# Scan layers of a four-layer kernel: B turned four times a pass, its diagonals made by VectorE straight from the scratch bank, and the second half's fills in another order

## The reference

```python
proj = seq @ W_proj.T + b_proj                     # x_in, delta, B, C
delta = softplus(delta + dt_bias)
h = exp(d_t * A) * h + (d_t * x_t) * b_t           # over the 1024 tokens, per channel and state
y_t = einsum('bdn,bn->bd', h, c_t)                 # C picks out of the 16 states
out = (y + x_in * D) @ W_out.T + b_out
```

## Time and profile before

| | |
|---|---|
| median of 3 runs | 4393.69 us (4382.99 to 4408.94) |
| the profiled execution | 4387.91 us, its span 4386.1 us |
| scans of the scan layers (line 1111) | first at 1808.9 us, last at 4361.1 us |
| PE busy | 3855.6 us, 88% |
| DVE busy | 3288.3 us, 75% |
| POOL busy | 2511.3 us, 57% |
| ACT busy | 2110.7 us, 48% |
| the diagonals (line 1135) | 128 instructions, 307.6 us |
| the copy to b_t (line 1002) | 32 instructions, 12.3 us |

### The profile page before, as it was taken

The page is one execution under the profiler, slowest core; times in us unless marked ns, Lnnn a source line. Parts: engine busy times, 40 slices in busy tenths (PEclk is TensorE's granted clock), DMA queues, the critical chain, the costliest instruction groups (busy, mean ns, idle before and its releaser), DMA issues.

```text
span 4386.1 us, 168626 instructions
## 1 busy us (share of the span) xinstructions
PE 3855.6 (88%) x73712; PEld 2419.1 (55%) x73712; DVE 3288.3 (75%) x3492; ACT 2110.7 (48%) x2771; POOL 2511.3 (57%) x877
## 2 busy tenths in 40 slices
PE   4994898999989984799999999999999999899997
PEld 4994666666666663345555455455555455455454
DVE  6555566666665762498888888888989788889887
ACT  2331444434434442455555555556565455555563
POOL 1121211211212110488888888888999788789888
PEclk9997899999999997699999999989999899899899
DMA  9624242332423321353453553543635435435433
GB/s 102 84 40 106 68 118 68 112 89 76 125 68 97 104 61 48 83 122 82 110 121 78 117 113 81 124 104 86 143 79 129 102 78 122 108 78 131 100 84 85
DMA packets 297043, 419.51 MB, mean 96 GB/s; under 512 B 31401, under 2 KB 185645, under 8 KB 296289
## 3 DMA queue, kind: packets, MB, share of 16 engines
q1 hardware_dynamic: 296322, 408.65, 41.7%
HBM read 267.06 MB, written 91.16 MB: 82 GB/s over the span
## 4 chain that ended last, share of the span: by engine, by line
PE 47%; issue 6%; DVE 5%; POOL 1%; ACT 1%; SPq 1%; DMA 0%; DVEq 0%; POOLq 0%; ACTq 0%
PE ssm_u_ps L801 18%; PE ssm_y_ps L814 16%; PE ssm_scratch L831 8%; DVE ssm_h L1111 3%; PE ssm_u_ps L874 2%; PE ssm_scratch L841 1%; PE ssm_scratch L856 1%; DVE ssm_b_diag L1135 1%; POOL ssm_h L1191 1%; SPq L735 1%; PE ssm_scratch L850 0%; ACT ssm_decay L948 0%; PE ssm_scratch L821 0%; DMA ssm_xn<-const_ones 0%; DVE ssm_y_sb L1140 0%
## 5 line engine op out<-in xcount | busy, mean ns | idle before, releaser
L1191 POOL TENSOR_TENSOR ssm_h<-ssm_h,ssm_c_rep 128x2048 f32<-128x2048 f32 x384 | 1741.8, 4540 | 176.7 <-DVE ssm_h L1111 160.6
L801 PEld LDWEIGHTS ssm_u_ps<-ssm_b_diag,ssm_dx_t 32*64 32x64 f32 x49152 | 842.3, 140 | 615.6 <-issue 612.6
L1111 DVE TENSOR_TENSOR_SCAN ssm_h<-ssm_decay,ssm_h,ssm_u_ps 128x512 f32<-128x512 f32 x768 | 945.7, 1259 | 191.2 <-PE ssm_u_ps L801 189.5
L801 PE MATMUL ssm_u_ps<-ssm_b_diag,ssm_dx_t 32*64 32x64 f32 x49152 | 947.4, 229 | 154.6 <-issue 111.1
L948 ACT ACTIVATE ssm_decay<-ssm_delta_rep,ssm_a_neg 128x1024 f32<-128x1024 f32 x768 | 861.7, 1144 | 381.3 <-DVE ssm_h L1111 374.8
L1111 DVE TENSOR_TENSOR_SCAN ssm_h<-ssm_decay,ssm_u_ps 128x512 f32<-128x512 f32 x768 | 887.8, 1196 | 60.9 <-PE ssm_u_ps L801 39.2
L814 PE MATMUL ssm_y_ps<-ssm_h,ssm_state_sum 128*64 128x512 f32 x3072 | 838.8, 670 | 15.1 <-POOL ssm_h L1191 8.0
L1725 ACT ACTIVATE l_probs<-l_work 128x532 f32<-128x532 f32 (+1 forms) x384 | 217.3, 566 | 559.7 <-PE l_work L1579 553.0
L814 PEld LDWEIGHTS ssm_y_ps<-ssm_h,ssm_state_sum 128*64 128x64 f32 x3072 | 202.7, 147 | 304.9 <-issue 267.4
L1894 DVE RECIPROCAL l_den<-l_den 96x1024 f32<-96x1024 f32 x32 | 209.6, 6549 | 195.5 <-ACT l_den L1738 195.5
L1977 POOL TENSOR_TENSOR l_rstd<-l_var_eps,l_minus_half 96x2 f32<-96x2 f32 x16 | 11.1, 693 | 585.9 <-DVE l_var_eps L1814 585.9
(11 more groups left out here) (162 smaller groups left out, 5644.2 us busy)
## 6 DMA issues: line engine op xcount, KB each, us to landing
ssm_c_rep<-ssm_c_by_state SPq DMA_DIRECT2D x256, 512.0 KB, 7.7
ssm_delta_rep<-ssm_delta SPq DMA_DIRECT2D x384, 128.0 KB, 6.3
l_qk_parts<-l_qk SPq DMA_DIRECT2D x48, 768.0 KB, 4.8
ssm_x<-x_after_l SPq DMA_DIRECT2D x32, 768.0 KB, 6.7
ssm_x_res<-x_after_l SPq DMA_DIRECT2D x192, 128.0 KB
l_x<-x SPq DMA_DIRECT2D x64, 192.0 KB, 9.0
x_after_l<-l_x SPq DMA_DIRECT2D x64, 192.0 KB, 4.1
l_x<-x_after_l SPq DMA_DIRECT2D x16, 768.0 KB, 5.3
```

The costliest lines, as they stand in the source:

```text
L801: made = nc.tensor.matmul(u_ps[64 * par:64 * par + 64, ring("u", w), r - 2 * win, at:at + 64], dx_t[rows, n.s, db, k, 64 * g:64 * g + 64], ...
L1111: nc.vector.tensor_tensor_scan(h[:, s % S_RING, npi, t], decay[:, 2 * (s % 2) + npi, t], u, start, ALU.mult, ALU.add).then_inc(scanned, 1)
L1191: nc.gpsimd.tensor_tensor(view, view, c_rep[:, 2 * q:2 * q + 2, :], ALU.mult).then_inc(c_applied, 1)
```

## The change

`bt` becomes four fills, `bt.0` to `bt.3`. PE makes the same four transposes for each of them, all of B each time. ACT's copy and the buffer `b_t` are gone: DVE's diagonal of group i waits for fill `bt.i`, reads the turned B in the PSUM bank `scratch` (one input in PSUM, `lane` in SBUF), and its end frees the bank (`drained` in place of `diag_made`). Twelve fills a pass become fifteen. In the second half of a pass `bc`, `x.0`, `de.1`, `de.2` and `dx.0` stand in earlier windows, and the four `bt.i` in windows 16, 18, 20 and 22. Lines below 462 move by one, lines behind 1000 by up to eight.

```diff
--- before.py
+++ after.py
@@ -459,7 +459,8 @@
 
 
     slots = {
-        1: ["x.2"], 2: ["dx.1"], 3: ["norm"], 6: ["dx.2"], 9: ["de.0"], 13: ["bc"], 14: ["bt"], 15: ["x.0"], 17: ["de.1"], 19: ["de.2"], 20: ["dx.0"], 21: ["x.1"],
+        1: ["x.2"], 2: ["dx.1"], 3: ["norm"], 6: ["dx.2"], 9: ["de.0"], 11: ["bc"], 13: ["x.0"], 14: ["de.1"],
+        16: ["bt.0"], 17: ["de.2"], 18: ["bt.1"], 19: ["dx.0"], 20: ["bt.2"], 21: ["x.1"], 22: ["bt.3"],
     }
     keep = lambda f: not first if f in OWN else not last
     return {slot: [f for f in names if keep(f)] for slot, names in slots.items()}
@@ -469,7 +470,7 @@
     return [f for names in slots.values() for f in names]
 
 
-FIRST_FILLS = ["norm", "de.0", "de.1", "de.2", "bc", "bt", "x.0", "x.1", "dx.0", "x.2", "dx.1", "dx.2"]
+FIRST_FILLS = ["norm", "de.0", "de.1", "de.2", "bc", "bt.0", "bt.1", "bt.2", "bt.3", "x.0", "x.1", "dx.0", "x.2", "dx.1", "dx.2"]
 MAIN_FILLS = flat(fill_order(False, False))
 EARLY = len(MAIN_FILLS) - len(flat(fill_order(True, False)))
 
@@ -513,7 +514,6 @@
         dx_t = sb("dx_t", [128, 2, 3, 4, 128])
         x_kept = sb("x_kept", [128, HALF])
         b_rows = sb("b_rows", [64, HALF])
-        b_t = sb("b_t", [128, 256])
         c_rows = sb("c_rows", [128, HALF])
         b_diag = sb("b_diag", [128, 4, 8, 2, 64])
         delta_rep = sb("delta_rep", [128, 3, L])
@@ -573,7 +573,6 @@
         delta_made = sem("delta_made")
         bc_kept = sem("bc_kept")
         dx_made = sem("dx_made")
-        diag_made = sem("diag_made")
         rows_seen = sem("rows_seen")
         window_free = sem("window_free")
         rep_free = sem("rep_free")
@@ -788,7 +787,7 @@
                     if npq == 0 and win == 0:
                         await_drained(pe, fill(n, f"dx.{db}"))
                     if db == 0 and win == 0:
-                        pe.wait_ge(diag_made, n.count(4, npq + 1))
+                        await_drained(pe, fill(n, f"bt.{npq}"))
                     if not (n.first and w < U_RING):
                         await_place(pe, n, "u", w)
                         pe.sem_inc(window_free, 1)
@@ -996,11 +995,6 @@
                     nc.scalar.activation(in_order(c_rows[64:128, :]), by_lane(scratch[64:128, :]),
                                          ACT.Copy).then_inc(drained, 1)
 
-                def take_b(n):
-                    f = fill(n, "bt")
-                    await_fill(act, f)
-                    nc.scalar.activation(b_t[:, :], scratch[:, 0:256], ACT.Copy).then_inc(drained, 1)
-
                 def take_x(n, db):
 
                     f = fill(n, f"x.{db}")
@@ -1029,14 +1023,14 @@
                     for name in slots(n).get(slot, ()):
                         kind, _, i = name.partition(".")
                         of = n if name in OWN else after(n)
+                        if kind == "bt":
+                            continue
                         if kind == "norm":
                             take_norm(of)
                         elif kind == "de":
                             take_delta(of, int(i))
                         elif kind == "bc":
                             take_bc(of)
-                        elif kind == "bt":
-                            take_b(of)
                         elif kind == "x":
                             take_x(of, int(i))
                         else:
@@ -1051,7 +1045,6 @@
                     for db in range(3):
                         take_delta(n, db)
                     take_bc(n)
-                    take_b(n)
                     take_x(n, 0)
                     take_x(n, 1)
                     take_dx(n, 0)
@@ -1127,13 +1120,12 @@
 
                 def diagonals(n, npq):
 
-                    if npq == 0:
-                        await_drained(dve, fill(n, "bt"))
-                    b = b_t[:, :].rearrange("p (c m) -> p c m", c=16)[:, :, 2 * npq:2 * npq + 2]
+                    await_fill(dve, fill(n, f"bt.{npq}"))
+                    b = scratch[:, 0:256].rearrange("p (c m) -> p c m", c=16)[:, :, 2 * npq:2 * npq + 2]
                     b = b[:, :, None, :].to_broadcast([128, 16, 32, 2])
                     m = lane[:, :].rearrange("p (j i) -> p j i", i=2)[:, None, :, :].to_broadcast([128, 16, 32, 2])
                     nc.vector.tensor_tensor(b_diag[:, npq].rearrange("p c a (j i) -> p (c a) j i", i=2), b, m,
-                                            ALU.mult).then_inc(diag_made, 1)
+                                            ALU.mult).then_inc(drained, 1)
 
                 def keep_y(n, db):
                     dve.wait_ge(y_summed, n.count(S_STEPS, 4 * db + 4))
```

## The result

The changed kernel takes 4647.69 us (median of 4 runs, 4637.63 to 4666.61), the kernel before, on the same chip, 4401.31 (4382.99 to 4409.67): slower, ratio 1.058 [1.055, 1.061]. The forecast was 4568 with a range to 4640: the direction held, the size did not. The profiled execution took 4653.84, 265.9 more than that of before.

What follows compares the result with a forecast made beforehand. PE was taken to set the pace up to window 17 and DVE from there; 4387.9 + 155 (31 passes of 5.0) + 7 (prologue) + 15 (clock) = 4565, set against the runs' median as 4568 us, range 4450 to 4640.

Steps and rivals of the forecast that it cites:

- The diagonal: DVE's diagonal from PSUM: 1.2 us in place of 2.39, four saving 4.9 us a pass.
- The start: Window 17, with bc earlier in PE's order: its fill ends later and DVE scans it 2.6 us later.
- the walk: Step through fill 14 to last diagonal with measured durations and new lists: 5.0 us more a pass; chance 0.63.
- The waits of 2.25 and 3.98: DVE's waits before diagonals 0 and 1: for bt.0 behind fill and sum, for bt.1 behind the relu of de.2.
- The rest of the pass: Windows after the next pass's first scan: run as before, with nothing left over on POOL and ACT.
- The prologue: Before the passes: four turns, each followed by a diagonal, in place of one turn and a copy; 7 us more.
- between nothing and 1.4 us a pass, I take 0.5: PE's clock after the 2.9 us wait before bt.1: 0.5 us a pass, 15 us in all.
- the rival given 0.10 (1.4 + 1): Clock stays low after new waits, or PE stalls hit DVE through bt.i: 1.4 + 1 us more a pass, 4628.
- What follows it contains waits of 0.4 and 0.6, which hide most: PE's waits after bt.1, for diagonal 1 and window 19's scan: said to hide most of the clock loss.
- just in time: bt.2 on PE, behind fill 22 and a sum: forecast at 87.28, with no DVE wait charged.
- Stalls of PE fall elsewhere in the pass: Fill 14 to last diagonal: 33.0 to 34.6 us in 30 stretches, so the walk was taken for all 31 passes.
- the rival at 4323: Faster: bt.0 and bt.1 full when DVE comes; 2.3 us a pass saved, 71 in all; chance 0.08.

Runs made afterwards that it cites:

- the first experiment: Changed kernel with POOL's second addition one step earlier, ahead of the apply_c of step 8: 4538.01 us, ratio 1.034.
- after, small C: Changed kernel with C loaded to one eighth of the columns from the second pass on: 4523.99 us, ratio 1.031.
- after, small C and filler: Changed kernel with C loaded to one eighth from the second pass on and three unread multiplications on PE before bt.1: 4483.44 us, ratio 1.021.
- The filler alone: Changed kernel with three multiplications that nobody reads, put on PE where it stands before bt.1: 4643.36 us, ratio 1.056.
- the small C alone: Kernel before with C loaded to one eighth from the second pass on: 4269.04 us, ratio 0.970; the same cut in the changed kernel: 4523.99.
- the same edit: POOL's second addition one step earlier: in the changed kernel 4538.01 us; in the kernel before with only the new fill order 4468.04, against 4468.16 without it.
- The first filler: Changed kernel with ten multiplications that nobody reads, put on PE before bt.1: 4747.27 us, ratio 1.080.

## Why the prediction was wrong in size

Right, by its own steps:
- **The diagonal.** 1.2 us forecast, 1.225 measured; POOL's additions 1.27 on average, as forecast. The saving is 4 x (2.45 - 1.22) = 4.9 us a pass, as summed. The Trainium skill's page "SBUF — State Buffer", section "Who interferes with whom", says that a VectorE instruction with one SBUF input does not contend with GpSimd, and one with two contends with a GpSimd instruction that reads SBUF; these rows agree. The Trainium skill's page "VectorE: DVE Perf Modes", section on the TRN2 errata, has a higher fixed cost from PSUM than from SBUF; none is seen here, since the shortest diagonal takes 1197 ns in either form.
- **The start.** The scan of window 17 comes 11.90 us behind the fill of window 14 (3177.89 - 3165.99), which is what the walk gives; before, it was 10.55, and that fill now comes behind `bc` as well.
- **The waits of 2.25 and 3.98**: 1.78 and 3.68 in the undisturbed pass, on the mean 1.73 and 4.23. The chain behind the second (scan, apply_c, addition, relu, bank) is as told, and the first experiment takes 2.6 us of it away.
- **The rest of the pass** costs the same. The prologue: 7 forecast; the first scan begins at 1813.27 in place of 1808.94, with a start 0.5 us earlier, so 4.8.

Wrong: **the step "between nothing and 1.4 us a pass, I take 0.5" for the clock, with the stalls of PE at nothing**. The stretch up to the last diagonal was to grow by 38.09 - 33.16 = 4.9 us and grew by 8.5 (41.89 - 33.41). The 30 stretches can be sorted by what happens in them (number of stretches, and the mean start of the last diagonal in us; "half clock to the end" are those without a stall in which the last diagonal waits over 5 us):

| kernel | undisturbed | a stall of PE over 1 us | half clock to the end |
|---|---|---|---|
| before | 23, 33.22 | 7, 34.02 | 0 |
| after | 12, 40.08 | 17, 42.96 | 1, 45.27 |
| after, small C | 17, 40.17 | 9, 41.85 | 4, 45.32 |
| after, small C and filler | 24, 38.40 | 3, 42.75 | 3, 44.73 |

In the undisturbed stretches the last diagonal comes 2.0 us later than the walk's 38.09. Of that the filler takes away 1.8 (40.17 to 38.40), so it is the half clock. The other stretches add 1.8 to the mean of 40.08. So 0.5 should have been 2.0 + 1.8, and the kernel before has 0.25 of its own (33.41 against 33.16): 3.55 us net, 3.05 more than charged, 95 us in 31 passes; the medians differ from the forecast by 80.

Both amounts were in the rival given 0.10 (1.4 + 1), and the measured 4648 lies nearest to that rival's 4628. The argument that kept the clock's share small was wrong at one place: "What follows it contains waits of 0.4 and 0.6, which hide most". Those waits of PE end with DVE's diagonal and scan, before the slow sum starts; the sum itself takes 1.7 us more, and `bt.2` right behind it was "just in time", with nothing in reserve.

The other half of the error is the lead. The prediction's "Stalls of PE fall elsewhere in the pass" was not so even before: in 7 of 30 stretches of the kernel before, PE came out of a stall over 1 us (1.6 on the mean), and the last diagonal was only 0.8 later for it: B had been turned long before, and no diagonal waited. With `bt.i` made just ahead of its diagonal that lead is gone: in its 17 disturbed stretches the stalls are 2.7 us on the mean and the last diagonal comes 2.9 later than in the 12 undisturbed ones. That more and longer stalls now fall into this stretch (0.54 us a pass before, 1.55 after) is measured; why is not known.

How much each is worth by itself stays open in part. The filler alone won 4 us, which is within the spread; the small C alone won as much in the kernel before. With the small C fewer of the changed kernel's stretches have a stall (9 in place of 17), but more run at half clock to the end (4 in place of 1), and the mean hardly moves. Only with both does the mean come down, to 39.47, and only the undisturbed stretches reach the forecast. What makes PE stall under the transfers wasn't tried; that fewer bytes for C cut the stalls is shown, why is not.

One sum of the prediction is off without weight: the rival at 4323 is 4394 - 71, without the prologue's 7 us that it names.

## What to carry to other kernels

When a change makes a producer's result just in time for a consumer that sets the pace, charge it with the producer's usual stalls and with the slow clock behind each new wait of TensorE, even if a walk with clean durations shows a fit: here that was 3.5 us a pass on top of the 5.0 that the walk had foreseen. Freeing an engine of 4.9 us a pass by reading PSUM in place of a second SBUF input was real, but it was spent by splitting one early turn into four late ones. Before taking a wait away ask what stands behind it: the same edit was worth 110 us where DVE depended on it and nothing where only PE did.

## What the runs showed of the hardware that was not expected

Here the half clock outlasted a wait by far, with no further gap behind it. PE in the changed kernel:

```profile
4174.43 0.59 PE L849 MATMUL ssm_scratch<-ssm_ident,ssm_b_rows 64*128 64x64 f32 x4 [2.85 <-ACT ssm_relu L985]
...
4185.97 3.68 PE L830 MATMUL ssm_scratch<-ssm_xn,ssm_w_x 97*64 97x512 f32 x8
4189.58 1.99 PE L800 MATMUL ssm_u_ps<-ssm_b_diag,ssm_dx_t 32*64 32x64 f32 x64
4191.49 3.66 PE L813 MATMUL ssm_y_ps<-ssm_h,ssm_state_sum 128*64 128x512 f32 x8
```

and its stretch:

```profile
4180.00:4195.00 15.00, 15.00 (x156) 6.22 (x156) 7.27 (x7) 4.51 (x5) 9.07 (x4) 0.50 0.51 123
```

PE is busy all 15 us at a granted clock of 0.50, and the last diagonal waits 5.61 us; in the pass at 3165.99 a wait of 2.84 cost one slow sum, and `bt.2` behind it was back at 0.46 us. With the small C this happened in 4 stretches of the changed kernel that had no stall over 1 us, and in 2 that had one.

The filler's multiplications, 64x512 like those of a `de` fill, took about twice as long each: three took 2.74 us, 0.91 each, where the four of a `de` fill take 1.87, 0.47 each. The first filler was mis-sized by that. In the program the four of a `de` fill write to partitions 0 to 63 and 64 to 127 in turn, the filler's always to 0 to 63; whether that makes the difference was not tried.
